# In the combination's steps, SP issues the next weight loads ahead of the output store and the x load

## The reference

```python
shared = jnp.einsum('ti,hi->th', jax.nn.silu(x @ sh_gate_w.T) * (x @ sh_up_w.T), sh_down_w)
probs = jax.nn.softmax((x @ router_weight.T).astype(jnp.float32), axis=-1)
top_v, top_i = jax.lax.top_k(probs, TOP_K)
top_v = top_v / top_v.sum(axis=-1, keepdims=True)
combine = (jax.nn.one_hot(top_i, E, dtype=top_v.dtype) * top_v[..., None]).sum(axis=1)
for e in range(E):
    gu = x @ gate_up_proj[e].T
    gate, up = (gu[:, :I_MOE], gu[:, I_MOE:])
    cur = jax.nn.silu(gate) * up @ down_proj[e].T
    out = out + cur * combine[:, e:e + 1]
out = out + jax.nn.sigmoid(x @ shared_gate_w.T) * shared
```

## Time and profile before

| what | us |
|---|---|
| median of 3 runs | 2139.0 |
| lowest and highest of them | 2136.22, 2146.01 |
| the profiled execution, device time | 2138.97 |
| its span, first to last instruction | 2136.5 |
| PE busy in it | 1983.1 (93%) |
| DVE busy | 1485.9 (70%) |
| ACT busy | 1164.0 (54%) |
| POOL busy | 748.4 (35%) |

### The profile page before, as it was taken

One profiled execution on the slowest core, in us unless ns is written; L12 is line 12 of the kernel. 1 busy time (PEld: TensorE's weight loads), 2 busy tenths in 40 slices (PEclk: granted clock), 3 DMA queues, 4 the chain that ended last, 5 costly groups with the idle time before them and its releaser, 6 DMA issues. The chain is left out here.

```text
span 2136.5 us, 32819 instructions
## 1 busy us (share of the span) xinstructions
PE 1983.1 (93%) x10142; PEld 1667.6 (78%) x10142; DVE 1485.9 (70%) x3511; ACT 1164.0 (54%) x2946; POOL 748.4 (35%) x1058
## 2 busy tenths in 40 slices
PE   7999999759999999999999999868999999999996
PEld 6677787537888888888888888756878888888775
DVE  7788547657766776767767777884467887774664
ACT  6742222336666666666666666643367776673332
POOL 3441001345555555555555555640600000001442
PEclk9999999869999999999999999978999999999998
DMA  7431110262000000000000000122689898884553
GB/s 253 137 130 51 42 36 20 99 243 96 21 11 21 10 0 30 0 20 10 20 10 20 10 1 6 65 69 87 239 315 327 315 322 309 306 307 156 170 187 109
DMA packets 82292, 244.78 MB, mean 115 GB/s; under 512 B 10464, under 2 KB 11104, under 8 KB 80256
## 3 DMA queue, kind: packets, MB, share of 16 engines
q1 hardware_dynamic: 77040, 226.46, 30.7%
q0 software_dynamic: 5120, 16.78, 2.3%
HBM read 207.81 MB, written 45.61 MB: 119 GB/s over the span
## 5 line engine op out<-in xcount | busy, mean ns | idle before, releaser
L269 PE MATMUL att_ps_xt<-att_w_hi,xT_hi 128*128 128x512 f32 x512 | 206.6, 404 | 28.2 <-DVE att_w_lo L2541 12.4
L2484 POOL TENSOR_SCALAR att_pr<-att_pr,att_ri 128x384 f32<-128x384 f32 (+2 forms) x256 | 136.5, 546 | 271.4 <-DVE att_ri L2579 271.4
L269 PE MATMUL att_ps_xt<-att_w_hi,xT_lo 128*128 128x512 f32 x512 | 204.5, 399 | 0.0
L269 PE MATMUL att_ps_xt<-att_w_lo,xT_hi 128*128 128x512 f32 x512 | 204.3, 399 | 0.0
L2677 ACT ACTIVATE att_pr<-att_pr,att_nb,att_r 128x384 f32<-128x384 f32 (+2 forms) x256 | 168.0, 659 | 36.8 <-DVE att_nb L2566 36.2
L2622 ACT ACTIVATE att_qkv<-att_ps_xt 128x512 f32<-128x512 f32 x128 | 76.3, 596 | 201.2 <-PE att_ps_xt L269 192.8
L1826 POOL DMA_INDIRECT y<-moe_rows,moe_slotA x16 | 16.0, 999 | 415.0 <-DMA moe_rows<-moe_lo_f 411.9
L2669 ACT ACTIVATE att_pT_hi<-att_ps_pt 128x768 fp32r<-128x768 f32 (+2 forms) x128 | 93.7, 732 | 122.7 <-PE att_ps_e L269 120.7
L269 PEld LDWEIGHTS att_ps_xt<-att_w_hi,xT_hi 128*128 128x128 f32 x512 | 97.6, 191 | 58.8 <-POOL att_w_lo L2457 23.2
L2489 POOL TENSOR_TENSOR att_rot<-att_rot 128x384 f32<-128x384 f32 x128 | 129.2, 1009 | 17.5 <-DVE att_rot L2532 17.5
L2549 DVE TENSOR_TENSOR att_q_lo<-att_ps_xt,att_q_hi 128x256 fp32r<-128x256 f32 x128 | 54.1, 423 | 112.9 <-ACT att_k_hi L2659 112.9
(11 more groups left out here) (329 smaller groups left out, 6682.6 us busy)
## 6 DMA issues: line engine op xcount, KB each, us to landing
y<-in_moe_rt SPq DMA_DIRECT2D x59, 704.0 KB, 6.5
y<-in_moe_rt SPq DMA_DIRECT2D x39, 768.0 KB, 6.5
moe_sraw_gu<-in_moe_sgu SPq DMA_DIRECT2D x44, 512.0 KB, 3.9
moe_sraw_d<-in_moe_sd SPq DMA_DIRECT2D x44, 256.0 KB, 4.2
moe_xs<-in_zeros SPq DMA_DIRECT2D x39, 256.0 KB, 9.4
moe_lo_f<-moe_xs SPq DMA_DIRECT2D x39, 256.0 KB, 6.7
moe_rows<-moe_lo_f SPq DMA_DIRECT2D x39, 256.0 KB, 6.6
att_raw_w<-in_qkv_w SPq DMA_DIRECT2D x8, 1024.0 KB, 4.8
```

The source lines that it names most:

```text
L269: mm = pe.matmul(out, lhsT, rhs, start=(i == 0), stop=(i == len(terms) - 1))
L2484: pool.tensor_scalar(p, p, ri[:, j % 2, g:g + 1], 1.0, ALU.mult, ALU.mult).then_inc(s("p"), 1)
```

## The change

SP goes over a list of its own, in which every step of the shared expert that follows a combination is moved in front of it. The other engines keep their list.

```diff
+def loads_first(items):
+
+    out = list(items)
+    for k in range(1, len(out)):
+        if out[k][0] == "S" and out[k - 1][0] == "C":
+            out[k - 1], out[k] = out[k], out[k - 1]
+    return out
...
             load_sgu(1)
-            for kind, n in items:
+            for kind, n in loads_first(items):
                 if kind == "S":
                     if n + 2 < N_SH:
                         load_sgu(n + 2)
```

## The result

| what | before | after |
|---|---|---|
| median, us (6 runs each) | 2138.84 | 2127.2 |
| lowest and highest | 2136.22, 2146.01 | 2124.31, 2131.32 |
| the profiled execution, us | 2138.97 | 2129.13 |
| its span | 2136.5 | 2126.8 |
| product of step 30 to that of step 40 on DVE (D) | 97.41 | 86.53 |

The ratio of the changed kernel to the kernel before is 0.9943, 95% interval 0.9925 to 0.9962: 11.6 us less at the medians. The interval is clear of 1, so the kernel is faster, and it reaches across the line of 0.5%.

A forecast was written before the change was run, and what follows sets the result against it. PE was taken as the bound, 8.39 us a step, with 11.7 us lost in steps 31 to 40. Terms of -10.8 and -0.2 us gave -11.0 against 2138.97: 2128.0 us, range 2124 to 2134.5.

The forecast's parts named there:

- (a): SP's gate weight load is issued when DVE's split ends, about 3.1 us earlier where the add was late.
- (b): Gate loads land within 6.2 us of the split, by 0.3 us at worst; ACT's waits in steps 31 to 40 go.
- (c): SP's down weight load is issued when DVE's down split ends, 2011.99, ahead of the add's end at 2013.58; costs nothing.
- (d): SP's store and load of x are issued as before, tile 15's load about 8 us later; costs nothing.
- (e): Gate split starts 0.2 us ahead of the second gather; steps take 8.30 us plus 0.14 for the product's low part, 8.44.
- (f): Next limit: DVE's loop, 0.05 us a step over PE's floor, and step 34 with ACT's scalings, 10.82 us.
- 2127.2 us for PE's floor: Total time if PE's floor bounded all steps but 34; said to be the least possible apart from the runs' spread.
- (2): Rival: POOL's second gather is never held, the add costs 0.96 us in nine steps; 2136.6 us, chance 0.05.
- (1): Rival: only ACT's waits for the load go, the add still falls on DVE's splits; 2131.9 us, chance 0.17.
- (3): Rival: gate loads land over 6.4 us after the split, each of ten steps takes 10.80 us; 2149.6 us, chance 0.03.
- (4): Rival: two stretches at TensorE's lower clock cost about 2 us; 2130 us, chance 0.08.
- (5): Rival: the change does nothing because the loads were hidden anyway; 2139 us, chance 0.05.

The follow-up runs named there:

- shared_behind: Changed kernel with ACT's four accumulator scalings of step 34 moved behind the SiLU; D 84.81 us, total 2128.09 us, ratio 0.9938 to the kernel before.
- traffic_only: Changed kernel with the store and load of x of one combination earlier put ahead of the gate load, without the add's wait; D 91.33 us, total 2135.42 us.
- gate_first: Kernel before with only the gate load moved ahead of store and load of x, the down load staying behind them; D 88.61 us, total 2132.32 us, one run.
- act_late: Changed kernel with one more ACT copy, 0.31 us, between norm and gate split in 12 combinations; D 98.36 us, total 2142.52 us, one run.
- late_noadd: act_late with POOL's add of x replaced by a memset of the same tile; D 88.47 us, total 2127.81 us, one run.
- wait_only: Changed kernel with the gate load waiting for the add of x, nothing in front of it; D 92.61 us, total 2131.81 us, ratio 0.9968 to the kernel before.

## Why the prediction was right

*What bounds it.* Right. 11.7 us were said to be lost in steps 31 to 40; 10.7 of them came back on PE. Of the 1.0 left over eleven floors, shared_behind takes 0.6, which were step 34's.

*(a), (b), in time.* Right in outcome: no load in steps 31 to 40 was late, in either profile. Its margin was read wrongly, to the safe side. The 0.3 us to spare came from a landing of 5.9 us that had a store and a load of x in front; with them 6.3 us was seen too (traffic_only), and without them, in gate_first, 4.1 at most.

*(c), (d), costs nothing.* Right; the store goes out with the add's end as before. But the down load, which I moved along with one sentence, is worth 2.1 us: gate_first has it late in one step of ten.

*(e), 0.14 a step.* Right. The low part of the product takes 0.74 to 0.84 us in the steps where I had put 0.83, the gather 1.83 to 1.86, and these steps 8.39 to 8.45. That the collision depends on an order of 0.2 us, and not on the lateness, was argued from three steps; act_late and late_noadd show it. "No split over 1.3 us" holds up to step 40, with 1.30 in step 34. In step 41 the gate split takes 1.54, in both kernels.

*(f) and the sum.* Step by step: 3 x 8.44 = 25.3 was 25.23, 10.82 was 10.83, 8.30 was 8.30, 5 x 8.44 = 42.2 was 42.17. D was forecast at 86.6 and is 86.53. Step 41 gave 0.19 on PE where 0.2 was put down, but it shouldn't have been added to a sum on DVE: from DVE's product of step 40 to the end of the span it is 45.24 us before and 45.27 after, so the terms give -10.8 us and not -11.0. The forecast stands beside -11.6 at the medians and -9.8 between the two profiled executions. The stage accounts for -10.9, and between the two profiled executions the rest lies ahead of step 30. Of that scatter traffic_only and wait_only give a measure: their totals are 3.2 and 6.8 us under the kernel before, and their D 6.1 and 4.8. A total within 1 us of the forecast is therefore in part luck; that D came within 0.1 us is not.

Three smaller readings were off. The four steps up to 40 don't simply repeat the pair: they took 8.31, 10.80, 8.30 and 11.29 us. The 2127.2 us for PE's floor doesn't follow from its rows: nine steps of 8.39 and one of 10.82 are 86.3 us, which gives 2127.9. Nor is that a limit, for step 34 can be shortened too (shared_behind). And 1.11 less 0.14 is 0.97 in rival (2), not 0.96.

*The rivals.* (1), only the waiting goes, would have been right if the collisions had stayed. They are gone, because they come with the order of gather and split. (2), the gather never held, is refuted by the held gather in all nine steps of both profiles. (3), slower, has its mechanism in act_late: D 98.4, through an operation on ACT and not through landings. (4), the clock: the granted clock was 1.00 in every stretch of 4 us from 1980 to 2100; the dip at 2054 us went with the gaps of PE. (5), no effect, is out by D.

What stays open is why loads with the same transfers in front land after 4.1 to 6.3 us (traffic_only, 2030 to 2045 us), how well D repeats where a load is near its margin, and what the stages ahead of step 30 did in the single executions.

## What to carry to other kernels

A queue that runs in program order should issue first what the next step on the critical loop reads, and behind it what only has to be done some time; each wait in front of such a load is paid in the slack between buffer free and buffer needed, here 6.2 us, and so are the transfers. Where VectorE and GpSimd alternate on the same SBUF data, look in the trace for the same instruction at two durations: here an order that 0.2 us decide was worth 1.1 to 1.3 us a step, and a load that was late by 0.2 us cost 1.5. And judge a change of ten us in two thousand by the distance between two marks in its own stage.

## What was not expected of the hardware

**A split gives way although it started first.** The Trainium skill, page "SBUF — State Buffer", section "Who interferes with whom", says, of DVE's modes that use two ports, that whoever of the two issues first keeps the shared ports for the whole instruction, and in general that the order of issue decides who is held. In step 36 of the kernel before DVE's gate split began at 2049.26 and the add 0.37 us later, with 1.31 us (timeline of POOL):

```profile
2049.63 1.31 POOL L1837 TENSOR_TENSOR y<-y,moe_hi_f 128x512 f32<-128x512 f32 x1
```

The add wasn't stretched and the split was, to 2.77 us, and ended 1.09 us after the add's end. With the add 0.09 to 0.42 us behind the start of the gate split this came in each of six steps in four kernels (2.48 to 2.82 us), and the down split of gate_first's step 40 gave way to an add 0.50 us behind it (2.34 us). With the add 0.8 to 1.0 us behind the gate split it comes out the page's way round: the split takes 1.22 to 1.28 us and the add is stretched to 1.42 to 1.57, then the down split waits for the add (1.78 to 1.79). Recorded starts may not be the moments at which the ports are taken; for the gate split no run has a case between 0.42 and 0.8.

**A gather is held by two-input subtractions.** The same section infers that they don't stop GpSimd's writing of descriptors. Here the second gather took 0.95 to 0.97 us when it was recorded ahead of the gate split or within 0.03 us of its start, and 1.83 to 1.94 when 0.13 to 0.23 us behind it, in steps 30 to 40 of every kernel that has the gather ahead of the add, also with the add replaced by the memset. In step 32, before and after, it ended 0.25 us after the down split. The gather also reads its row numbers (moe_slotB), so it may be this read that is held and not the writing of descriptors; no run separates the two. The hold is what puts the add out of harm's way in the changed kernel.
